# Linear attention: context times output weights first, then queries times the folded weights

## The chip, the cores and the metric

One core of a Trainium2 chip runs the whole program. Its engines work side by side, each through its own queue in order, and meet at semaphores: TensorE (PE; its weight loads are PEld), VectorE (DVE), ScalarE (ACT), GpSimd (POOL) and SyncE (SP). The metric is the device time of one execution in microseconds.

## The reference

A decoder of two layers, on x of shape (2, 1024, 256), that is 2 batches of 1024 tokens and 256 features, all in 32-bit floats. Each layer has a self attention, a cross attention with a small context, and a third part. The change lies in the first part alone, a pre-norm linear attention with 4 heads of 64 and a feed-forward net:

```
h = layer_norm(x, ln1_g, ln1_b)
q, k, v = (h @ wq, h @ wk, h @ wv), each split in 4 heads of 64
q = softmax(q * scale, over the 64 features of the head)
k = softmax(k * scale, over the 1024 tokens)
context = einsum('bhnd,bhne->bhde', k, v)
attn    = einsum('bhnd,bhde->bhne', q, context)
x = x + attn @ wo + bo
h = layer_norm(x, ln2_g, ln2_b)
x = x + gelu(h @ w_ff1 + b_ff1) @ w_ff2 + b_ff2
x = x @ w_d + b_d
```

## The kernel before

The program is written engine by engine: four layer functions, each one block with a list of instructions per engine, in an order set by hand. `linear_attention_layer` is the first of them. It treats the two batches b = 0 and 1 in an interleaved order. Activations lie feature by token: FT = 2 tiles of 128 features, with 1024 tokens in NCH = 2 chunks of 512. Queries and values are made token by feature (4 units u of two 128-token tiles, 256 features each). Each batch has four PSUM banks of 128x512 floats, `bank(b, 0)` to `bank(b, 3)`.

For each batch, the steps between the two norms are:

- `keys` (TensorE), `max_keys` (VectorE, L650), `exp_keys` (ScalarE, L518): the keys, feature by token, and exp of them shifted by their maximum. The exp leaves the sum over tokens in k_s. The division by that sum comes later.
- `values` and `queries` (TensorE, both through `by_token`, L343), copied by `copy_values` (VectorE, L659), or shifted by the maximum of each head (`shift_queries`, VectorE: L665 reduces, L667 subtracts), then `exp_queries` (ScalarE, L524) and `normalise_queries` (VectorE: L673 sum, L675 reciprocal, L677 multiply).
- `turn_keys` (TensorE, L358) transposes exp(keys), and `copy_keys` (ScalarE, L530) moves them to SBUF. `turn_queries` (L376) and `copy_queries` (L537) do the same for the queries, the other way round.
- `contexts` (TensorE, L366): for each of 2 head pairs a 128x128 product over the 1024 tokens. `copy_context` (VectorE, L690) takes the two 64x64 blocks on its diagonal and multiplies them by 1/k_s; the rest of the tile `context` stays zero.
- `attend` (TensorE, L385): context times queries, 4 products of 128x512. `copy_attended` (ScalarE, L544) copies them to SBUF.
- `project` (TensorE, L393): the output weights a_wo times the attended values, 8 products. `add_attended` (VectorE: L698 adds bias and residual, L701 the two halves for the mean).
- The second norm: `mean` (L314), `centre` (L619), `square` (ScalarE, L495), `variance` (L325), `roots` (ScalarE, L509 and L512), `normalise` (VectorE, L626 and L629). For batch 1 the squares are made on VectorE (`fold_squares`, L728 and L730), and `folded_variance` (L319) takes them.
- The feed-forward part runs in units: `widen(u)` (L407), `gelu(u)` (L559, L561), `narrow(u)` (L418), with weights and activations split in a rounded part and a rest, by three products each. ScalarE makes the rounded parts (`split_w` L547, `split_h2` L552), GpSimd the rests (`leave_w` L290, `leave_h2` L295, L307 for the activations). TensorE runs `mean` of batch 1 after widen(2) and `folded_variance` after widen(5).

Every product of plain 32-bit floats appears as two MATMUL instructions in the trace, so 16 products are x32; a transpose of 128x128 and a product of rounded operands (fp32r) appear as one.

The orders that matter here:

- TensorE: ... queries(1), attend(0), turn_keys(1), project(0), turn_queries(1), mean(0), contexts(1), variance(0), attend(1), project(1), widen(0) ...
- VectorE: ... normalise_once(1), copy_context(0), shift_queries(1), normalise_queries(1), add_attended(0), centre(0), copy_context(1), normalise(0), add_attended(1), centre(1) ...
- ScalarE: ... copy_queries(0), exp_queries(1), copy_attended(0), copy_keys(1), split_w(0, 2, 3), copy_queries(1), split_w(1), square(0), roots(0), copy_attended(1), split_h2(0), gelu(0) ...
- GpSimd: leave_w(0, 2, 3, 1), leave_h2(0) for both chunks, then the rests of the activations.

SyncE issues only two loads of later weights in this layer (L282), and they are done well before the stretch of the change.

Of the kernel before, what the change touches and what calls it, by code (L numbers as in the profile page):

```python
# [24 lines left out]
ALU = mybir.AluOpType  # L25
ACT = mybir.ActivationFunctionType
AX = mybir.AxisListType.X

P = 128
B, S, D = 2, 1024, 256  # L30
T = B * S
FT = D // P
CH = 512
NCH = S // CH
TT = S // P
# [64 lines left out]
class Chip:  # L100
# [52 lines left out]
    def bank(self, i):  # L153
        return self.psum[i // 2][:, (i % 2) * CH:(i % 2 + 1) * CH]
# [29 lines left out]
def linear_attention_layer(nc, c):  # L184

    DH = 64
# [10 lines left out]
    with ExitStack() as ctx:  # L197
# [3 lines left out]
        sg = [c.signals(nc, f"a{b}", dict(  # L201
            k_proj=4, k_step=7, k_shift=1, k_exp=4, k_turned=4, k_copied=4, v_proj=4, v_copied=4,
            q_proj=4, q_step=12, q_shift=4, q_exp=4, q_norm=4, q_turned=4, q_copied=4,
            ctx_done=1, ctx_copied=1, at_done=4, at_copied=4, o_done=4, y_done=4,
            y2_done=4, d_done=4)) for b in range(B)]
        ff = c.signals(nc, "ff", dict(done=UNITS, act=2 * UNITS, rest=UNITS, narrowed=FT * UNITS, split=1, left=1, squared=1))
        parts = [("w", i) for i in (0, 2, 3, 1)] + [("h", b, j) for b in range(B) for j in range(NCH)]
# [2 lines left out]
        zeroed = sems.enter_context(nc.semaphore("a_zeroed"))  # L210
# [7 lines left out]
        k_r = sb("a_k_r", [P, B, FT])  # L218
        q_m = sb("a_q_m", [P, B, 4, 8])
        q_s = sb("a_q_s", [P, B, 4, 8])  # L220
        context = sb("a_context", [P, B, FT, P])
# [3 lines left out]
        room = lambda b, i: arenas[b][:, i * FT * S:(i + 1) * FT * S]  # L225
        tiles = lambda b, i: room(b, i).rearrange("p (m t) -> p m t", m=FT)
        h1, h2, centred, squares = ([tiles(b, i) for b in range(B)] for i in range(4))
        ek = qt = [tiles(b, 4) for b in range(B)]
        v_t = [room(b, 3).rearrange("p (t n) -> p t n", t=TT) for b in range(B)]
        ekt_t = [room(b, 2).rearrange("p (t n) -> p t n", t=TT) for b in range(B)]  # L230
        q_t = [room(b, 5).rearrange("p (u n) -> p u n", u=4) for b in range(B)]
        at = [tiles(b, 5) for b in range(B)]
        y = h1
        round_tiles = lambda b, i: arenas_round[b][:, i * FT * S:(i + 1) * FT * S].rearrange("p (m t) -> p m t", m=FT)
        h2_high, h2_rest = ([round_tiles(b, i) for b in range(B)] for i in (3, 1))
# [25 lines left out]
        bank = lambda b, i: c.bank(4 * b + i)  # L261
        col = lambda j: slice(j * CH, (j + 1) * CH)
# [12 lines left out]
        with nc.Block() as block:  # L275
# [34 lines left out]
            def _(pe):  # L310
# [10 lines left out]
                def variance(b, s):  # L321
                    for j in range(NCH):
                        pe.wait_ge(*s["sq"](j + 1))
                        for k in range(FT):
                            mm = pe.matmul(bank(b, 2 * j + 1), c.mean_w[:], squares[b][:, k, col(j)], start=(k == 0), stop=(k == 1))  # L325
                        mm.then_inc(s["var"].sem)
# [23 lines left out]
                def queries(b):  # L350
                    by_token(b, "a_wq", sg[b]["v_copied"], sg[b]["q_proj"])

                def turn_keys(b):
                    for u in range(4):
                        pe.wait_ge(*sg[b]["q_shift"](u + 1))
                        for t in (0, 1):
                            for m in range(FT):
                                mm = pe.transpose(bank(b, u)[:, t * D + m * P:t * D + (m + 1) * P],  # L358
                                                  ek[b][:, m, (2 * u + t) * P:(2 * u + t + 1) * P], c.ident[:])
                        mm.then_inc(sg[b]["k_turned"].sem)  # L360

                def contexts(b):
                    pe.wait_ge(*sg[b]["q_copied"](1))
                    for m in range(FT):
                        for t in range(TT):
                            mm = pe.matmul(bank(b, 0)[:, m * P:(m + 1) * P], ekt_t[b][:, t, m * P:(m + 1) * P],  # L366
                                           v_t[b][:, t, m * P:(m + 1) * P], start=(t == 0), stop=(t == TT - 1))
                    mm.then_inc(sg[b]["ctx_done"].sem)

                def turn_queries(b):  # L370
# [6 lines left out]
                                                  q_t[b][:, u, t * D + m * P:t * D + (m + 1) * P], c.ident[:])  # L377
                        mm.then_inc(sg[b]["q_turned"].sem)

                def attend(b):  # L380
                    pe.wait_ge(*sg[b]["ctx_copied"](1))
                    pe.wait_ge(*sg[b]["q_copied"](4))
                    for j in range(NCH):
                        for m in range(FT):
                            pe.matmul(bank(b, 2 * j + m), context[:, b, m, :], qt[b][:, m, col(j)],  # L385
                                      start=True, stop=True).then_inc(sg[b]["at_done"].sem)

                def project(b):
                    for j in range(NCH):
                        pe.wait_ge(*sg[b]["at_copied"](2 * (j + 1)))  # L390
                        for m in range(FT):
                            for k in range(FT):
                                mm = pe.matmul(bank(b, 2 * j + m), c.w("a_wo", k, m * P, P), at[b][:, k, col(j)],  # L393
                                               start=(k == 0), stop=(k == 1))
                            mm.then_inc(sg[b]["o_done"].sem)

# [53 lines left out]
                values(1)  # L450
                turn_queries(0)
                contexts(0)
                queries(1)
                attend(0)
                turn_keys(1)
                project(0)
                turn_queries(1)
                mean(0, ln2[0])
                contexts(1)
                variance(0, ln2[0])  # L460
                attend(1)
                project(1)
                for n in range(UNITS + LAG):
                    if n < UNITS:
# [26 lines left out]
            def _(act):  # L491
# [14 lines left out]
                def roots(b, s, eps, scale=1.0):  # L506
                    for j in range(NCH):
                        act.wait_ge(*s["var"](j + 1))
                        act.activation(factor(b, j), bank(b, 2 * j + 1), ACT.Ln, bias=eps[:, 0:1], scale=scale).then_inc(s["log"].sem)  # L509
                    for j in range(NCH):  # L510
                        act.wait_ge(*s["log"](j + 1))
                        act.activation(factor(b, j), factor(b, j), ACT.Exp, scale=-0.5).then_inc(s["rstd"].sem)  # L512
# [8 lines left out]
                def exp_queries(b):  # L521
                    for u in range(4):
                        act.wait_ge(*sg[b]["q_shift"](u + 1))
                        act.activation(q_t[b][:, u, :], q_t[b][:, u, :], ACT.Exp, scale=SCALE).then_inc(sg[b]["q_exp"].sem)  # L524

                def copy_keys(b):
                    act.wait_ge(*ln1[b]["once"](NCH))
                    for u in range(4):
                        act.wait_ge(*sg[b]["k_turned"](u + 1))
                        act.activation(ekt_t[b][:, 2 * u:2 * u + 2, :].rearrange("p t n -> p (t n)"), bank(b, u), ACT.Copy)\  # L530
                           .then_inc(sg[b]["k_copied"].sem)
# [5 lines left out]
                        act.activation(qt[b][:, :, u * D:(u + 1) * D], bank(b, u).rearrange("p (m n) -> p m n", m=FT),  # L537
                                       ACT.Copy).then_inc(sg[b]["q_copied"].sem)

                def copy_attended(b):  # L540
                    for j in range(NCH):
                        for m in range(FT):
                            act.wait_ge(*sg[b]["at_done"](2 * j + m + 1))
                            act.activation(at[b][:, m, col(j)], bank(b, 2 * j + m), ACT.Copy).then_inc(sg[b]["at_copied"].sem)  # L544

                def split_w(i):
                    act.activation(w_high[i], w_raw[i], ACT.Copy).then_inc(split["w", i].sem)  # L547

                def split_h2(b):
                    for j in range(NCH):  # L550
                        act.wait_ge(*ln2[b]["out"](FT * (j + 1)))
                        act.activation(h2_high[b][:, :, col(j)], h2[b][:, :, col(j)], ACT.Copy).then_inc(split["h", b, j].sem)  # L552
# [32 lines left out]
                copy_keys(0)  # L585
                copy_queries(0)
                exp_queries(1)
                copy_attended(0)
                copy_keys(1)
                act.wait_ge(c.first_loaded, 48)  # L590
                for i in (0, 2, 3):
# [3 lines left out]
                split_w(1)  # L595
                square(0, ln2[0])
                roots(0, ln2[0], c.eps)
                copy_attended(1)
                split_h2(0)
                for u in range(UNITS):  # L600
                    gelu(u)
# [9 lines left out]
            def _(dve):  # L611
# [66 lines left out]
                           .then_inc(sg[b]["q_norm"].sem)  # L678

                def copy_context(b):  # L680
                    dve.wait_ge(*sg[b]["k_exp"](4))
                    dve.tensor_tensor(k_r[:, b, :], k_s[:, b, :, 0], k_s[:, b, :, 1], ALU.add).then_inc(sg[b]["k_step"].sem)
                    dve.wait_ge(*sg[b]["k_step"](6))
                    dve.reciprocal(k_r[:, b, :], k_r[:, b, :]).then_inc(sg[b]["k_step"].sem)
                    dve.wait_ge(*sg[b]["k_step"](7))
                    dve.wait_ge(zeroed, 1)
                    dve.wait_ge(*sg[b]["ctx_done"](1))
                    for m in range(FT):
                        for h in (0, DH):
                            ins = dve.tensor_scalar(context[h:h + DH, b, m, h:h + DH], bank(b, 0)[h:h + DH, m * P + h:m * P + h + DH],  # L690
                                                    k_r[h:h + DH, b, m:m + 1], None, ALU.mult)
                    ins.then_inc(sg[b]["ctx_copied"].sem)

                def add_attended(b):
                    for j in range(NCH):
# [2972 lines left out]
def wait_for_weights(nc, c):  # L3668

    with nc.Block() as block:  # L3670

        @block.sync
        def _(sync):
            sync.wait_ge(c.first_loaded, 48)
            sync.wait_ge(c.others_loaded, B * 16)


LAYERS = [linear_attention_layer, cross_attention_and_recurrence, causal_attention_layer,
          context_attention_layer]

# [60 lines left out]
```

## Time and profile before

| | |
|---|---|
| time before, median of 3 runs | 1552.42 us (1550.23 to 1552.64) |
| the profiled execution, its own time | 1552.19 us |
| its span (first to last instruction) | 1550.4 us |
| PE busy | 1458.8 us, 94% |
| DVE busy | 988.1 us, 64% |
| ACT busy | 762.3 us, 49% |
| POOL busy | 454.1 us, 29% |
| mean granted TensorE clock | 0.983 of full |
| first layer's attention up to the first widen | 0 to 113.3 us of the span |

Times are counted from the start of the span. Busy shares are averages over all four layer functions. A row of the timeline gives the start, the time until the end of the last of the merged instructions, the engine, the line, what is written and read, the count, and in brackets the idle time of that engine just before it, with what ended it.

### The profile page before, as it was taken

How to read it: one execution, taken by the hardware profiler on the slowest of the kernel's cores; microseconds unless marked ns; L12 is line 12 of the kernel's file. 1: busy time of each engine (PE TensorE's matmuls, PEld its weight loads, DVE VectorE, ACT ScalarE, POOL GpSimd, SP SyncE). 2: the span in 40 equal slices, each digit the busy share in tenths (PEclk: the TensorE clock that was granted, in tenths of full speed). 3: DMA queues.
4: the chain of work that ended last, by engine and by line, in shares of the span. 5: the costliest groups of instructions: out<-in, count | busy, mean ns of one | idle time of the engine just before them, and what ended most of it. 6: DMA issues, size and time to landing. Idle time of an engine off the chain costs nothing. (4 is left out here: it accounts for less than half of the span.)

```text
span 1550.4 us, 19613 instructions
## 1 busy us (share of the span) xinstructions
PE 1458.8 (94%) x7170; PEld 859.1 (55%) x7170; DVE 988.1 (64%) x1506; ACT 762.3 (49%) x1317; POOL 454.1 (29%) x348
## 2 busy tenths in 40 slices
PE   6999999989999899879999999899889999999998
PEld 3757765423232365444545443323568888888886
DVE  5774244778877634448887773677577574664753
ACT  5566345533434642725666665434655544445442
POOL 0046430142221410370000000201236656655562
PEclk9999999999999999989999999999999999999999
DMA  7000000000000000191553300000413222223201
GB/s 292 1 0 0 1 4 1 0 1 1 1 1 0 1 0 1 48 142 16 132 68 50 43 2 1 4 1 0 137 41 106 72 82 100 78 70 107 73 10 55
DMA packets 39047, 67.59 MB, mean 44 GB/s; under 512 B 3944, under 2 KB 19368, under 8 KB 38568
## 3 DMA queue, kind: packets, MB, share of 16 engines
q1 hardware_dynamic: 38952, 66.33, 16.1%
q8 instruction: 58, 0.95, 0.3%
q14 instruction: 37, 0.30, 0.1%
HBM read 57.80 MB, written 8.39 MB: 43 GB/s over the span
## 5 line engine op out<-in xcount | busy, mean ns | idle before, releaser
L2232 ACT ACTIVATE arena<-psum 128x512 f32<-128x512 f32 (+3 forms) x384 | 164.7, 498 | 118.8 <-PE psum L2082 85.1
L2277 DVE TENSOR_REDUCE b_mx<-psum 128x1 f32<-128x512 f32 (+3 forms) x304 | 181.4, 653 | 57.0 <-PE psum L2058 47.4
L3021 POOL TENSOR_TENSOR m_w_rest<-m_w,m_w_high 128x512 fp32r<-128x512 f32 (+1 forms) x88 | 111.6, 1270 | 154.7 <-ACT m_w_high L3220 154.7
L3471 DVE TENSOR_TENSOR m_hidden<-m_gelu,psum 128x512 f32<-128x512 f32 (+1 forms) x88 | 60.4, 686 | 147.7 <-ACT m_gelu L3312 124.5
L3114 PE MATMUL psum<-m_x_high,m_w_high 128*128 128x512 f32 (+1 forms) x352 | 137.9, 392 | 3.2 <-issue 3.2
L3027 POOL TENSOR_TENSOR m_h_rest<-m_hidden,m_h_high 128x512 fp32r<-128x512 f32 (+1 forms) x88 | 122.1, 1388 | 59.0 <-ACT m_h_high L3234 59.0
L3114 PE MATMUL psum<-m_x_rest,m_w_high 128*128 128x512 f32 (+1 forms) x352 | 137.7, 391 | 0.0
L3114 PE MATMUL psum<-m_x_high,m_w_rest 128*128 128x512 f32 (+1 forms) x352 | 137.6, 391 | 0.0
L3312 ACT ACTIVATE m_gelu<-psum 128x512 f32<-128x512 f32 (+1 forms) x88 | 52.4, 596 | 119.7 <-PE psum L3114 119.7
L1359 ACT ACTIVATE x_probs<-psum 128x1024 f32<-128x1024 f32 x56 | 57.3, 1023 | 90.4 <-PE psum L1097 90.4
L1517 DVE TENSOR_REDUCE x_mx<-psum 128x2 f32<-128x1024 f32 x64 | 76.6, 1218 | 35.0 <-PE psum L1071 34.8
L3234 ACT ACTIVATE m_h_high<-m_hidden 128x512 fp32r<-128x512 f32 (+1 forms) x88 | 55.7, 633 | 82.7 <-DVE m_hidden L3471 82.7
L2079 PE MATMUL psum<-b_q_stack,b_k_stack 98*128 98x512 bf16 (+3 forms) x288 | 89.9, 331 | 5.5 <-DMA b_q_stack<-b_stage 3.1
L2055 PE MATMUL psum<-b_k_stack,b_q_stack 96*128 96x512 bf16 (+3 forms) x288 | 87.1, 332 | 4.8 <-DVE b_mx L2277 2.1
L1994 POOL TENSOR_TENSOR weights_sb<-weights_sb 128x1024 f32<-128x1024 f32 x3 | 5.7, 1892 | 271.0 <-DVE weights_sb L2332 271.0
L3114 PEld LDWEIGHTS psum<-m_x_high,m_w_high 128*128 128x128 f32 (+1 forms) x352 | 65.3, 185 | 18.4 <-issue 3.6
L3114 PEld LDWEIGHTS psum<-m_x_high,m_w_rest 128*128 128x128 f32 (+1 forms) x352 | 65.4, 186 | 15.2
L3114 PEld LDWEIGHTS psum<-m_x_rest,m_w_high 128*128 128x128 f32 (+1 forms) x352 | 65.4, 186 | 15.1
L2094 PE MATMUL psum<-arena,weights_sb 128*32 128x512 f32 (+3 forms) x768 | 73.3, 500 | 0.0
L3127 PE MATMUL psum<-m_h_high,m_o_high 128*128 128x512 f32 (+1 forms) x176 | 72.3, 411 | 0.2 <-POOL m_h_rest L3027 0.2
L3127 PE MATMUL psum<-m_h_high,m_o_rest 128*128 128x512 f32 (+1 forms) x176 | 68.8, 391 | 0.0
L3127 PE MATMUL psum<-m_h_rest,m_o_high 128*128 128x512 f32 (+1 forms) x176 | 68.7, 390 | 0.0
(594 smaller groups left out, 3252.7 us busy)
## 6 DMA issues: line engine op xcount, KB each, us to landing
m_w<-w SPq DMA_DIRECT2D x32, 512.0 KB, 4.5
m_wo<-wo SPq DMA_DIRECT2D x16, 512.0 KB, 4.0
weights_sb<-weights SPq DMA_DIRECT2D x2, 2820.0 KB, 12.3
m_w<-w SPq DMA_DIRECT2D x16, 344.0 KB, 4.6
b_q_stack<-b_q_dram SPq DMA_DIRECT2D x36, 128.0 KB, 6.0
b_k_stack<-b_k_dram SPq DMA_DIRECT2D x36, 128.0 KB, 5.9
weights_sb<-weights SPq DMA_DIRECT2D x1, 3328.0 KB, 14.3
b_q_dram<-b_q_parts SPq DMA_DIRECT2D x6, 512.0 KB, 3.4
```

The costliest lines, as they stand in the source:

```text
L1359: ins = act.activation(probs[slot % RING][:], two_heads(units), ACT.Exp, scale=SCALE)
L1517: dve.tensor_reduce(mx[:, n % 2, i // 2, i % 2, :], two_heads(tile(("piece", n, i))), AX, ALU.max).then_inc(s["read"].sem)
L2055: mm = pe.matmul(bank[:, x * keys:(x + 1) * keys], qs[n % 3][0:ROWS, h, qi * P:(qi + 1) * P], ks[n % 3][0:ROWS, h, first:first + keys], st ...
L2079: mm = pe.matmul(score(slot)[:, 0:n], ks[a][0:ROWS + SHIFT, h, ki * P:(ki + 1) * P], qs[a][0:ROWS + SHIFT, h, q0:q0 + n], start=True, stop ...
L2094: mm = pe.matmul(out_tile[h * PAD:(h + 1) * PAD, CH - n:CH], v_aug[:, b * TT + ki, quad * QUAD + h, :], probs[(QUAD * (2 * pair + i) + h) ...
L2232: act.activation(probs[slot % RING][:, 0:n], score(slot)[:, 0:n], ACT.Exp, scale=SCALE).then_inc(s["expd"].sem)
L2277: dve.tensor_reduce(mx[:, part, qi, heads[0]:heads[0] + nh], tile(("piece", p))[:, 0:nh * keys].rearrange("p (h n) -> p h n", n=keys), AX, ...
L3021: pool.tensor_tensor(w_rest[:, n % W_RING, :, :, 0:H_N(n % HT)], raw_of(n), w_high[:, n % W_RING, :, :, 0:H_N(n % HT)].bitcast(F32), ALU.s ...
L3027: pool.tensor_tensor(h_rest[rows, n % H_RING, :], hidden[rows, n % 2, :], h_high[rows, n % H_RING, :].bitcast(F32), ALU.subtract).then_inc ...
L3114: mm = pe.matmul(c.bank(base + n % 2)[0:H_N(h), :], of[:, k, :], x_of[ex % 2][:, k, :], start=(k == 0 and i == 0), stop=(k == FT - 1 and i ...
L3127: mm = pe.matmul(total(m), of[rows, n % O_RING, m * P:(m + 1) * P], h_of[rows, n % H_RING, :], start=(h == 0 and i == 0), stop=(h == HT - ...
L3471: dve.tensor_tensor(hidden[rows, n % 2, :], gelu[rows, n % 2, :], c.bank(2 + n % 2)[rows, :], ALU.mult)\
```

## The change

Before, the queries q are multiplied by the context C and the result by the output weights: (q C) Wo. After, the context is multiplied by the output weights first, and the queries by that product: q (C Wo).

- `contexts` swaps its two operands, so that the context comes out transposed, values by keys.
- `copy_context` copies the four diagonal blocks as they are. Then it forms 1/k_s, waits for `folded`, and writes `fold`, 128x256 for each head pair, from bank(b, 1), multiplied by 1/k_s.
- `attend` and `copy_attended` are gone. `fold_context` takes attend's place on TensorE: two products of 128x256. `project` waits for `fold_copied` and for all of `q_copied`, and takes `fold` as stationary and the queries as moving operand.
- `fold` lies in the first 512 columns of the room that held the attended values.

```diff
@@ contexts
-                            mm = pe.matmul(bank(b, 0)[:, m * P:(m + 1) * P], ekt_t[b][:, t, m * P:(m + 1) * P],
-                                           v_t[b][:, t, m * P:(m + 1) * P], start=(t == 0), stop=(t == TT - 1))
+                            mm = pe.matmul(bank(b, 0)[:, m * P:(m + 1) * P], v_t[b][:, t, m * P:(m + 1) * P],
+                                           ekt_t[b][:, t, m * P:(m + 1) * P], start=(t == 0), stop=(t == TT - 1))
@@ TensorE
-                def attend(b):
+                def fold_context(b):
+
                     pe.wait_ge(*sg[b]["ctx_copied"](1))
+                    pe.wait_ge(*sg[b]["q_copied"](2))
+                    for m in range(FT):
+                        mm = pe.matmul(bank(b, 1)[:, m * D:(m + 1) * D], context[:, b, m, :], c.w("a_wo", m, 0, D),
+                                       start=True, stop=True)
+                    mm.then_inc(sg[b]["folded"].sem)
+
+                def project(b):
+                    pe.wait_ge(*sg[b]["fold_copied"](1))
                     pe.wait_ge(*sg[b]["q_copied"](4))
                     for j in range(NCH):
                         for m in range(FT):
-                            pe.matmul(bank(b, 2 * j + m), context[:, b, m, :], qt[b][:, m, col(j)],
-                                      start=True, stop=True).then_inc(sg[b]["at_done"].sem)
-
-                def project(b):
-                    for j in range(NCH):
-                        pe.wait_ge(*sg[b]["at_copied"](2 * (j + 1)))
-                        for m in range(FT):
                             for k in range(FT):
-                                mm = pe.matmul(bank(b, 2 * j + m), c.w("a_wo", k, m * P, P), at[b][:, k, col(j)],
+                                mm = pe.matmul(bank(b, 2 * j + m), fold[b][:, k, m * P:(m + 1) * P], qt[b][:, k, col(j)],
                                                start=(k == 0), stop=(k == 1))
                             mm.then_inc(sg[b]["o_done"].sem)
@@ order on TensorE
-                attend(0)
+                fold_context(0)
                 turn_keys(1)
                 project(0)
...
-                attend(1)
+                fold_context(1)
                 project(1)
@@ ScalarE
-                def copy_attended(b):
-                    for j in range(NCH):
-                        for m in range(FT):
-                            act.wait_ge(*sg[b]["at_done"](2 * j + m + 1))
-                            act.activation(at[b][:, m, col(j)], bank(b, 2 * j + m), ACT.Copy).then_inc(sg[b]["at_copied"].sem)
...
-                copy_attended(0)
...
-                copy_attended(1)
@@ VectorE
                 def copy_context(b):
+                    dve.wait_ge(zeroed, 1)
+                    dve.wait_ge(*sg[b]["ctx_done"](1))
+                    for m in range(FT):
+                        for h in (0, DH):
+                            ins = dve.tensor_copy(context[h:h + DH, b, m, h:h + DH], bank(b, 0)[h:h + DH, m * P + h:m * P + h + DH])
+                    ins.then_inc(sg[b]["ctx_copied"].sem)
                     dve.wait_ge(*sg[b]["k_exp"](4))
...
                     dve.wait_ge(*sg[b]["k_step"](7))
-                    dve.wait_ge(zeroed, 1)
-                    dve.wait_ge(*sg[b]["ctx_done"](1))
+                    dve.wait_ge(*sg[b]["folded"](1))
                     for m in range(FT):
-                        for h in (0, DH):
-                            ins = dve.tensor_scalar(context[h:h + DH, b, m, h:h + DH], bank(b, 0)[h:h + DH, m * P + h:m * P + h + DH],
-                                                    k_r[h:h + DH, b, m:m + 1], None, ALU.mult)
-                    ins.then_inc(sg[b]["ctx_copied"].sem)
+                        ins = dve.tensor_scalar(fold[b][:, m, :], bank(b, 1)[:, m * D:(m + 1) * D], k_r[:, b, m:m + 1], None, ALU.mult)
+                    ins.then_inc(sg[b]["fold_copied"].sem)
```

## Rows read from the trace of the kernel before

**Rows 1.** The page: busy time, share of span and count per engine.
```profile
PE 1458.8 (94%) x7170; PEld 859.1 (55%) x7170; DVE 988.1 (64%) x1506; ACT 762.3 (49%) x1317; POOL 454.1 (29%) x348
```

**Rows 2.** Timeline of TensorE, 71 to 114 us: start, length, operation, count, idle before.
```profile
71.73 7.07 PE L343 MATMUL psum<-weights_sb,a_arena 128*128 128x256 f32 x32
78.64 3.60 PE L385 MATMUL psum<-arena,a_context 128*128 128x512 f32 x8
82.07 1.91 PE L358 MATMUL psum<-ident,a_arena 128*128 128x128 f32 x16
83.82 7.03 PE L393 MATMUL psum<-arena,weights_sb 128*128 128x512 f32 x16
...
94.42 1.12 PE L314 MATMUL psum<-ln,mean_w 128*128 128x512 f32 x2 [0.96 <-DVE ln L701]
...
102.39 3.60 PE L385 MATMUL psum<-a_arena,a_context 128*128 128x512 f32 x8
106.76 7.13 PE L393 MATMUL psum<-a_arena,weights_sb 128*128 128x512 f32 x16 [0.78 <-ACT a_arena L544]
113.33 1.03 PE L407 MATMUL psum<-arena_round,ln_round 128*128 128x512 f32 x2
```

**Rows 3.** Timeline of VectorE, 51 to 106 us.
```profile
51.09 0.69 DVE L667 TENSOR_TENSOR arena<-psum,a_q_m 128x512 f32<-128x512 f32 x1
51.70 0.68 DVE L665 TENSOR_REDUCE a_q_m<-psum 128x8 f32<-128x512 f32 x1
52.41 0.69 DVE L667 TENSOR_TENSOR arena<-psum,a_q_m 128x512 f32<-128x512 f32 x1
...
64.68 2.63 DVE L659 COPY a_arena<-psum 128x512 f32<-128x512 f32 x4
...
72.03 1.18 DVE L690 TENSOR_SCALAR a_context<-psum,a_k_r 64x64 f32<-64x64 f32 x4 [2.05 <-PE psum L366]
...
79.57 0.69 DVE L667 TENSOR_TENSOR a_arena<-psum,a_q_m 128x512 f32<-128x512 f32 x1
...
85.80 0.69 DVE L677 TENSOR_TENSOR a_arena<-a_arena,a_q_s 128x512 f32<-128x512 f32 x1
...
90.89 0.75 DVE L698 SCALAR_TENSOR_TENSOR arena<-psum,vectors_sb,arena 128x512 f32<-128x512 f32 x1 [0.96 <-PE psum L393]
91.67 2.69 DVE L701 TENSOR_TENSOR ln<-arena 128x512 f32<-128x512 f32 x1
...
105.25 0.75 DVE L626 SCALAR_TENSOR_TENSOR arena<-arena,vectors_sb,ln 128x512 f32<-128x512 f32 x1 [4.82 <-ACT ln L512]
```

**Rows 4.** Timeline of TensorE at folded_variance of batch 1.
```profile
127.28 1.13 PE L319 MATMUL psum<-a_arena,mean_w 128*128 128x512 f32 x2 [1.05 <-DVE a_arena L730]
```

**Rows 5.** Timeline of ScalarE, 80 to 86 us.
```profile
80.29 0.63 ACT L524 ACTIVATE a_arena<-a_arena 128x512 f32<-128x512 f32 x1 [1.10 <-DVE a_arena L667]
80.83 2.04 ACT L544 ACTIVATE arena<-psum 128x512 f32<-128x512 f32 x4
82.77 2.06 ACT L530 ACTIVATE a_arena<-psum 128x512 f32<-128x512 f32 x4
84.69 1.08 ACT L547 ACTIVATE ln_round<-weights_sb 128x1024 fp32r<-128x1024 f32 x1
```

**Rows 6.** GpSimd's timeline and line L290 (shortest, median, longest ns), VectorE's L701.
```profile
85.86 2.87 POOL L290 TENSOR_TENSOR weights_sb_round<-weights_sb,ln_round 128x1024 fp32r<-128x1024 f32 x1 [80.86 <-ACT ln_round L547]
L290 POOL TENSOR_TENSOR weights_sb_round<-weights_sb,a_w_high x2: 2352/2580/2808, 88.7 to 91.5; 128x1024 fp32r<-128x1024 f32 x2
88.24 1.03 DVE L701 TENSOR_TENSOR ln<-arena 128x512 f32<-128x512 f32 x1
```

**Rows 7.** Timeline of GpSimd at the rest of h2, batch 0.
```profile
108.87 2.88 POOL L295 TENSOR_TENSOR arena_round<-arena,arena_round 128x1024 fp32r<-128x1024 f32 x1 [12.03 <-ACT arena_round L552]
```

**Rows 8.** Busy time by stretch: PE, PEld, DVE, ACT, POOL, then granted clock.
```profile
20.00:22.00 2.00, 0.47 (x1) 0.30 (x2) 1.85 (x3) 1.97 (x4) 0.00 (x0) 1.00 0.75 180
22.00:26.00 4.00, 4.00 (x7) 1.66 (x6) 3.89 (x8) 3.60 (x5) 0.00 (x0) 0.57 1.05 451
```

More of the change, by code:

```diff
@@ L203, in linear_attention_layer @@
             q_proj=4, q_step=12, q_shift=4, q_exp=4, q_norm=4, q_turned=4, q_copied=4,
-            ctx_done=1, ctx_copied=1, at_done=4, at_copied=4, o_done=4, y_done=4,
+            ctx_done=1, ctx_copied=1, folded=1, fold_copied=1, o_done=4, y_done=4,
             y2_done=4, d_done=4)) for b in range(B)]
@@ L231, in linear_attention_layer @@
         q_t = [room(b, 5).rearrange("p (u n) -> p u n", u=4) for b in range(B)]
-        at = [tiles(b, 5) for b in range(B)]
+        fold = [room(b, 5)[:, 0:FT * D].rearrange("p (m n) -> p m n", m=FT) for b in range(B)]
         y = h1
```

## The prediction

> **What bounds the kernel now.** Start with the page [rows 1]. TensorE is busy 94% of the span, which suggests that any work taken off it shortens the run. That is an average over four layers; the change touches only the first, so I read that layer's stretch, 64 to 130 us, engine by engine in order of time.
>
> TensorE's own timeline comes first [rows 2]. From 71.73 us its pieces follow each other without idle time through queries(1), attend(0), turn_keys(1) and project(0). Then come two short waits: 0.96 us for DVE's second sum ahead of the ln2 mean, and 0.78 us for ACT's copy of the attended values ahead of project(1). widen(0) follows project(1) at 113.33. So TensorE is the bound here, but others are close behind. VectorE's timeline [rows 3] shows how close: in add_attended(0) DVE waits for TensorE by only 0.96 us, and its second sum L701 ends at 91.67 + 2.69 = 94.36, which releases the mean at 94.42. A chain hangs on that sum: mean, centring, square, variance, roots, normalise(0), the split of h2, widen(0); and on DVE itself add_attended(1) and the squares for folded_variance(1), for which TensorE again waits 1.05 us at 127.28 [rows 4]. From the second sum on, DVE's chain and TensorE's stream are within about 1 us of each other.
>
> **Part by part.** *Removed from TensorE:* attend, 8 instructions of 512 columns per batch. The row of attend(0) runs from 78.64 to the start of turn_keys(1) at 82.07: 3.43 us, twice [rows 2]. *Added:* fold_context, two matmuls of 256 columns, 4 instructions. queries(1) has 32 of that form in 78.64 - 71.73 = 6.91 us [rows 2], 0.216 each, so 0.86 us. Net -2.57 us a batch, -5.1 us in all, if nothing else moved. contexts only swaps its operands, 128 columns either way, and project has the same 16 instructions with another stationary matrix: both cost what they did.
>
> *Removed from ScalarE:* the eight copies of copy_attended, 82.77 - 80.83 = 1.94 us a batch [rows 5]. ACT is not the bound at batch 0; at batch 1 the copies are what project(1) waits for (the 0.78 us).
>
> *VectorE:* four context copies of 64x64 stay (1.18 us for four [rows 3]); copy instead of multiply I cost at nothing, since both read 64 columns of PSUM. They no longer wait for the reciprocal, which is done in time anyway. New are two multiplications 128x256 out of PSUM, a form that the trace does not have. Bounds: 0.30 us apart for 64 columns (1.18 over four) and 0.65 apart for the 512 columns of copy_values (2.63 over four) [rows 3]. The slope between them gives 0.45 each, the value that I take: 0.90 us for the pair, bounds 0.6 to 1.3. The Trainium skill ("VectorE: DVE Perf Modes", the section on the TRN2 errata) gives 120 + 256 cycles at 0.96 GHz, an estimate of 0.39 us each; by that page the sum would be 0.1 us lower.
>
> *The wait.* This is what counts. copy_context(0) now ends with a wait for folded, and fold_context(0) stands on TensorE behind all of queries(1). On DVE shift_queries(1) is queued behind that wait, then normalise_queries(1) and add_attended(0). Before, DVE shifted each quarter of the queries as TensorE delivered it, the last at 79.57 [rows 3]. Now:
> - the fold starts at 78.64, ends at 78.64 + 3 x 0.216 + 0.37 (what the last of queries(1) takes, 7.07 - 31 x 0.216) = 79.67; the pair of multiplications runs 79.70 to 80.60;
> - four quarters of shift_queries(1) at 52.41 - 51.09 = 1.32 us, 0.71 of it the maximum L665 [rows 3]: the last L667 begins at 80.60 + 3 x 1.32 + 0.71 = 85.28, where it began at 79.57: 5.7 us later;
> - turn_keys(1), which needs each quarter, no longer starts at once: it is paced by DVE, its last quarter goes at 86.0, and project(0) starts at about 86.45 instead of 83.82, in spite of the 2.57 us saved. It ends at about 93.4, its second product at 90;
> - normalise_queries(1): its last L677 began 85.80 - 79.57 = 6.23 us after the last L667 [rows 3], four quarters of 1.56. Undisturbed, DVE is through with it at 92.1 (it was at 86.4). add_attended(0) then no longer waits for project(0), and its four products (some 0.77 each) and two sums (some 0.65 each) end at 96.5, 2.1 us later than now;
>
> *The move against GpSimd.* ACT's copy_keys(1) stands behind exp_queries(1), so the splits of the weights move too: before, exp of the last quarter at 80.29, eight copies, split at 84.69, L290 at 85.86 [rows 5, 6]; now exp at 86.0, four copies, first split at 86.0 + 0.54 + 1.92 = 88.5, and GpSimd's first L290 1.17 later, at 89.64. The rows show what happens when a DVE operation with two SBUF inputs meets a GpSimd one [rows 3, 6]: L701 at 91.67 takes 2.69 instead of 0.69 and ends 0.55 us after GpSimd's third L290 (91.5 + 2.35), while GpSimd's second, at 88.68, takes 2.81 because L701 of 88.24 is running. One waits for the other to finish. The skill has the same rule ("SBUF — State Buffer", "Who interferes with whom"): such a DVE instruction and a GpSimd instruction that reads SBUF hold the same port in turn. Before, the queries were normalised before GpSimd began at 85.86 (one L677 at its edge). Now they are not. I alternate the two queues, each L290 2.35 us alone and 2.22 after a DVE operation, each DVE operation 0.55 after a release:
> - L290 first 89.64 to 92.0; the third L677, due at 89.96, ends at 92.55 (L290 comes first by 0.3 us);
> - L290 second to 94.77; the fourth L677, due 93.41, ends at 95.32;
> - L290 third to 97.54; first L701, due 96.78, ends at 98.09;
> - L290 fourth, ready at 97.7, to 100.31; second L701, due 99.56, ends at 100.86.
> The second sum is thus 100.86 - 94.36 = 6.5 us later.
>
> *After the sum.* The chain through mean, contexts(1), variance, roots and normalise(0) is unchanged and moves by 6.5. For batch 1 the wait for folded(1) is covered: the fold follows variance(0) (102.39 before), DVE has its product 2.0 us later, at 104.4 in old time, and it would idle until 105.25 anyway [rows 3]; if that cover failed, normalise(0) would pay the difference. project(1) starts at 104.4 in old time instead of 106.76, 2.3 us sooner; but widen(0) needs GpSimd's rest of h2, ready at 108.87 + 2.88 = 111.75 [rows 7], so only 113.33 - 111.75 = 1.6 us are gained at widen(0), and TensorE gives them back at the mean and folded variance of batch 1, which hang on DVE's chain. I put 0 of them in the sum, bound -1.6. Nothing later in the kernel waits for a clock of its own, so the shift stays to the end.
>
> Sum, against the profiled execution's 1552.19 us (span 1550.4 and 1.8 around it; the median is 0.2 above): 1552.19 + 6.5 = 1558.7 us.
>
> **Rivals.**
> - *B, the port costs less.* If the third L677 wins against the first L290 (0.3 us decide), the second sum comes 4.8 us late: 1557.0. With no collisions at all it is 2.1: 1554.3, no change that can be told. For it: the margin is small. Against it: both starts hang on the same L667, so it does not scatter much. Less the up to 1.6 of widen(0), this case spans 1553 to 1557.
> - *C, the clock falls as well.* In 20 to 22 us TensorE was busy for 0.47 us of 2, at 2.4 GHz; in the 4 us that follow, full of work, the granted clock is 0.57 on average, that is mostly at 1.2 GHz [rows 8]. In the new order TensorE has little to do from 79.7 to 86.4 and again from 94.8 to 100.9. A fall in the first stretch slows project(0), which has some 3 us of cover (its second product is needed at 96). A fall in the second slows contexts(1), which the variance waits for. In the 4 us of the row 0.43 x 4 = 1.7 us of clock were lost: 1560.4. Against it: both stretches hold short pieces of work.
> - *D, faster.* TensorE's stream sets the end and the wait is absorbed: 1552.19 - 5.1 = 1547.1. It takes a DVE that is ahead of TensorE by more than the stall. DVE waited for project(0) by 0.96 us [rows 3]; the stall of 5.7 us would have to be under about 1.3. It would need the fold to be released before the end of queries(1), against TensorE's order. The change not doing what it says gives a time within this case and the old one.
>
> **How the numbers follow.** Forecast 0.57, B 0.22, C 0.16, D 0.05. The forecast's own range is 1557 to 1560 (0.3 on either side for the new DVE operation, -1.6 for widen(0), and for GpSimd's queue falling otherwise in the feed-forward part). For 8 in 10 I reach down to most of B, 1555.0, and up over C, 1561.5. A measurement of this kernel can tell about 0.2%, 3.1 us, from no change. Faster by more: D without the failed-to-apply part, 0.04. Within: B's end without collisions and the rest of D, 0.11. Slower: 0.85.
>
> **What would show it.** In the profile of the changed kernel: DVE idle about 6 us before its first 128x256 multiplication, released by the fold; turn_keys(1) in four pieces 1.32 us apart; the third and fourth L677 near 2.6 and 1.9 us instead of 0.69, and GpSimd's L290 beginning near 89.6; the second L701 ending near 100.9; project(1) following the fold by about 1 us without ACT between. The prediction is wrong if shift_queries(1) starts before 79 us, if L677 and L290 overlap without growing, or if TensorE does not wait for DVE's two sums between 94.8 and 101.

## The result and the profile after

The changed kernel takes 1561.47 us (median of 6 runs, 1558.44 to 1565.27) against 1552.26 us for the kernel before in the same comparison. The ratio is 1.0064, with a 95% interval of 1.0051 to 1.0077: 0.64% slower, or 1.0064 x 1552.2 = 1562.1 us. The forecast was 1558.7 us. Its direction, the wait and the collisions hold; the loss is 9.9 us where 6.5 were forecast, because TensorE's clock fell twice and the sum had no term for it.

The profiled execution took 1564.93 us with a span of 1562.0 us, 11.6 more than before. TensorE's timeline at the change, the rows that answer to [rows 2]:

```profile
71.82 7.07 PE L343 MATMUL psum<-weights_sb,a_arena 128*128 128x256 f32 x32
78.73 1.03 PE L385 MATMUL psum<-weights_sb,a_context 128*128 128x256 f32 x4
82.11 0.66 PE L358 MATMUL psum<-ident,a_arena 128*128 128x128 f32 x4 [2.36 <-DVE a_arena L661]
83.44 1.11 PE L358 MATMUL psum<-ident,a_arena 128*128 128x128 f32 x4 [0.67 <-DVE a_arena L661]
...
87.00 8.67 PE L395 MATMUL psum<-arena 128*128 128x512 f32 x16
95.50 1.91 PE L376 MATMUL psum<-ident,a_arena 128*128 128x128 f32 x16
98.17 1.12 PE L314 MATMUL psum<-ln,mean_w 128*128 128x512 f32 x2 [0.76 <-DVE ln L698]
102.22 2.07 PE L314 MATMUL psum<-ln,mean_w 128*128 128x512 f32 x2 [2.92 <-DVE ln L698]
104.08 5.30 PE L366 MATMUL psum<-a_arena 128*128 128x128 f32 x32
109.22 3.60 PE L325 MATMUL psum<-arena,mean_w 128*128 128x512 f32 x8
112.65 1.03 PE L385 MATMUL psum<-weights_sb,a_context 128*128 128x256 f32 x4
114.72 7.13 PE L395 MATMUL psum<-a_arena 128*128 128x512 f32 x16 [1.04 <-DVE a_arena L688]
```

Up to 78.73 nothing has changed. The fold takes four instructions where attend took eight. Then turn_keys(1), which had run through in one piece, comes in pieces, each behind an L661 of DVE (the old L667); the first piece takes 0.66 us, the second, with the same work, 1.11. project(0) takes 8.67 us where it took 7.03, and contexts(1) 5.30 where it took 3.73. Both wear the mark of a slower TensorE. Before, contexts(1) and the variance behind it were:

```profile
95.38 3.73 PE L366 MATMUL psum<-a_arena 128*128 128x128 f32 x32
98.95 3.60 PE L325 MATMUL psum<-arena,mean_w 128*128 128x512 f32 x8
```

VectorE's timeline, which answers to [rows 3]; L661 is the old L667, L667 the old L673, L671 the old L677, L698 the old L701:

```profile
79.86 0.87 DVE L688 TENSOR_SCALAR arena<-psum,a_k_r 128x256 f32<-128x256 f32 x2 [6.46 <-PE psum L385]
80.66 0.68 DVE L659 TENSOR_REDUCE a_q_m<-psum 128x8 f32<-128x512 f32 x1
...
85.34 0.69 DVE L661 TENSOR_TENSOR a_arena<-psum,a_q_m 128x512 f32<-128x512 f32 x1
...
90.01 2.58 DVE L671 TENSOR_TENSOR a_arena<-a_arena,a_q_s 128x512 f32<-128x512 f32 x1
92.51 0.67 DVE L667 TENSOR_REDUCE a_q_s<-a_arena 128x8 f32<-128x512 f32 x1
...
93.45 1.89 DVE L671 TENSOR_TENSOR a_arena<-a_arena,a_q_s 128x512 f32<-128x512 f32 x1
...
96.70 1.42 DVE L698 TENSOR_TENSOR ln<-arena 128x512 f32<-128x512 f32 x1
98.04 1.40 DVE L695 SCALAR_TENSOR_TENSOR arena<-psum,vectors_sb,arena 128x512 f32<-128x512 f32 x2
99.47 2.69 DVE L698 TENSOR_TENSOR ln<-arena 128x512 f32<-128x512 f32 x1
```

DVE idles 6.46 us for the fold. The third and fourth L671 take 2.58 and 1.89 us, and both sums are drawn out too, the second to 99.47 + 2.69 = 102.16. GpSimd's timeline, which answers to [rows 6], shows what they meet:

```profile
89.67 2.36 POOL L290 TENSOR_TENSOR weights_sb_round<-weights_sb,ln_round 128x1024 fp32r<-128x1024 f32 x1 [84.67 <-ACT ln_round L543]
92.00 5.57 POOL L290 TENSOR_TENSOR weights_sb_round<-weights_sb,a_w_high 128x1024 fp32r<-128x1024 f32 x2
99.28 2.34 POOL L290 TENSOR_TENSOR weights_sb_round<-weights_sb,arena_round 128x1024 fp32r<-128x1024 f32 x1 [1.71 <-ACT arena_round L543]
```

And the busy time by stretch (columns as in [rows 8]) has the clock: 0.50 of full, the lower level of 1.2 GHz, in two stretches just behind or among TensorE's waits for DVE.

```profile
80.00:84.00 4.00, 1.22 (x7) 0.98 (x8) 3.91 (x7) 1.22 (x2) 0.00 (x0) 0.93 0.00 0
84.00:88.00 4.00, 3.58 (x13) 2.26 (x12) 3.88 (x7) 2.62 (x6) 0.00 (x0) 0.50 0.00 0
102.00:106.00 4.00, 3.78 (x11) 2.75 (x12) 2.64 (x5) 1.41 (x2) 0.00 (x0) 0.50 0.00 0
```

To tell parts of a few us from each other, I read each profile between two marks: the first instruction behind queries(1) on TensorE (attend(0) or the fold, "the mark"), and the first DVE product that takes the feed-forward total of batch 0 (L705 before, L702 after). What lies ahead of the mark varies by 2.3 us from profile to profile (the mark lies between 76.44 and 78.73); the mean clock of whole runs varies too (0.975 to 0.985 of full). Two profiles of the changed kernel ("after" and "after_again") differ by 0.2 us in these readings. Before and after, the second mark is:

```profile
147.60 1.44 DVE L705 SCALAR_TENSOR_TENSOR arena<-psum,vectors_sb,arena 128x512 f32<-128x512 f32 x2 [0.92 <-PE psum L418]
```
```profile
157.98 1.46 DVE L702 SCALAR_TENSOR_TENSOR arena<-psum,vectors_sb,arena 128x512 f32<-128x512 f32 x2 [0.89 <-PE psum L420]
```

That is 147.60 - 78.64 = 68.96 us before and 157.98 - 78.73 = 79.25 after: 10.3 us of the loss lie here, against 9.9 for whole runs. All runs, with those two readings (each from one profile, less the kernel before) beside the ratio of whole runs:

| run | second sum ends, from the mark | between the marks | ratio [95%] |
|---|---|---|---|
| before | 15.72 | 68.96 | 1 |
| after | +7.7 | +10.3 | 1.0064 [1.0051, 1.0077] |
| after_again | +7.6 | +10.1 | 1.0063 [1.0048, 1.0078] |
| hold | +2.7 | +3.5 | 1.0029 [1.0017, 1.0041] |
| move | +0.9 | +3.7 | 1.0021 [1.0011, 1.0030] |
| both | -3.0 | -2.9 | 0.9987 [0.9975, 0.9998] |
| fill | +6.4 | +6.5 | 1.0041 [1.0028, 1.0054] |
| fold0_only | +7.5 | +9.9 | 1.0056 [1.0038, 1.0074] |
| fold1_only | 0.0 | +0.1 | 0.9992 [0.9976, 1.0009] |
| before_hold | -2.0 | -1.3 | 0.9994 [0.9984, 1.0005] |
| both_later | -3.0 | -5.3 | 0.9973 [0.9959, 0.9988] |
| before_hold_later | -2.0 | -2.6 | 0.9975 [0.9960, 0.9990] |

### The profile page after: what moved, and what is told of

It is laid out like the page before. It is cut to its first block and busy times, and to the rows that moved or that the text cites. A ratio compares the mean times of both kernels' runs of the same rounds, so it can differ in the third digit from the quotient of the medians.

```text
span 1562.0 us, 19593 instructions
## 1 busy us (share of the span) xinstructions
PE 1462.1 (94%) x7158; PEld 861.6 (55%) x7162; DVE 992.9 (64%) x1510; ACT 758.0 (49%) x1309; POOL 453.5 (29%) x348
```

## The experiments

Theory: the changed kernel loses by DVE's wait for the fold, by the collisions between DVE and GpSimd into which this wait pushes them, and by TensorE's clock. Rivals: one of the three does it alone, or the loss lies elsewhere.

**The changed kernel again**, as the mark for its neighbours.

> The changed kernel once more, as the mark beside which the next three are read. Its trace so far has the second sum of the second norm ending at 102.2 us (94.4 before) and the clock at 1.2 GHz in two stretches, 83 to 90 and 101 to 107 us. Theory (the DVE wait, the port shared with GpSimd, and the clock together): 1558 to 1565 us in single runs, middle near 1561. Rival (what was first seen was a chance state of the clock in that one profile): middle at 1557 or below.

Measured: 1562.97 us, ratio 1.0063. Its profile has both collisions and both stretches at 1.2 GHz again, so they were not a chance of the first profile.

**hold**: GpSimd starts on the weights only after both sums.

```diff
+                pool.wait_ge(*ln2[0]["sum"](NCH))
                 for i in (0, 2, 3, 1):
                     leave_w(i)
```

> The changed kernel, with GpSimd's four subtractions for the weights held back until DVE has made both sums ahead of the second norm (one wait more on GpSimd, nothing left out). DVE still waits for the fold. Theory: no L677 or L701 takes over 0.8 us; the last quarter of the queries is normalised at 92.1 instead of 95.3, the second sum ends near 97 instead of 102.2; TensorE is not idle for long before the mean, so the second fall of the clock goes too: 1555 us, 6 less than the changed kernel. Rival (the port costs nothing on the path, the wait alone does it): 1561, as the changed kernel. Second rival (the subtractions are now late for widen(0)): over 1561.

Measured: 1556.48 us, 6.5 less than the changed kernel beside it (6 expected). VectorE's timeline, then TensorE's:

```profile
90.54 0.69 DVE L672 TENSOR_TENSOR a_arena<-a_arena,a_q_s 128x512 f32<-128x512 f32 x1
...
94.58 0.75 DVE L696 SCALAR_TENSOR_TENSOR arena<-psum,vectors_sb,arena 128x512 f32<-128x512 f32 x1 [0.65 <-PE psum L396]
95.37 0.69 DVE L699 TENSOR_TENSOR ln<-arena 128x512 f32<-128x512 f32 x1
```
```profile
85.96 8.59 PE L396 MATMUL psum<-arena 128*128 128x512 f32 x16
94.38 1.91 PE L377 MATMUL psum<-ident,a_arena 128*128 128x128 f32 x16
96.13 1.88 PE L315 MATMUL psum<-ln,mean_w 128*128 128x512 f32 x4
97.85 3.73 PE L367 MATMUL psum<-a_arena 128*128 128x128 f32 x32
```

DVE's products and both sums are back at 0.69. The first fall of the clock is still there (project(0) 8.59 us), and DVE now waits 0.65 us for it; that is why the second sum is 2.7 us late and not the 2.1 worked out. The second fall is gone, and with it TensorE's waits at the means. Holding GpSimd back thus takes off 6.8 of the 10.3 us. Not all of that is the change's own: the kernel before has collisions too [rows 6], and the run "before_hold" below shows that the same edit takes 1.3 us off it between the marks.

**move**: DVE scales the fold of batch 0 after it has shifted the queries of batch 1.

```diff
                 copy_context(0)
                 shift_queries(1)
+                scale_fold(0)
                 normalise_queries(1)
...
                 copy_context(1)
+                scale_fold(1)
```

(scale_fold is the end of copy_context, from the wait for folded on.)

> The changed kernel, with the two multiplications of the fold of batch 0 moved behind shift_queries(1) on DVE (batch 1 as it was; nothing left out). Theory: DVE shifts each quarter as TensorE delivers it, the last at 79.6; the fold is scaled at 80.3 to 81.1; turn_keys(1) has no gaps and the first stretch at 1.2 GHz is gone. GpSimd's subtractions now begin 2 us sooner than in the kernel before, near 83.9, and meet the third and fourth L677 and both sums: second sum near 95.4, 1.1 later than before: 1553. Rival (with the wait gone, the 5 us that TensorE saves show in full): 1547.

Measured: 1554.94 us, expected 1553. VectorE, GpSimd and TensorE:

```profile
83.96 1.91 DVE L671 TENSOR_TENSOR a_arena<-a_arena,a_q_s 128x512 f32<-128x512 f32 x1
...
86.74 1.90 DVE L671 TENSOR_TENSOR a_arena<-a_arena,a_q_s 128x512 f32<-128x512 f32 x1
```
```profile
82.83 2.49 POOL L290 TENSOR_TENSOR weights_sb_round<-weights_sb,ln_round 128x1024 fp32r<-128x1024 f32 x1 [77.84 <-ACT ln_round L543]
```
```profile
80.18 7.03 PE L395 MATMUL psum<-arena 128*128 128x512 f32 x16
...
91.45 1.12 PE L314 MATMUL psum<-ln,mean_w 128*128 128x512 f32 x2 [2.11 <-DVE ln L699]
94.21 2.08 PE L314 MATMUL psum<-ln,mean_w 128*128 128x512 f32 x2 [1.63 <-DVE ln L699]
96.08 5.51 PE L366 MATMUL psum<-a_arena 128*128 128x128 f32 x32
```

Without the wait the first fall is gone (project(0) 7.03), and the second sum is only 0.9 late, as forecast (1.1). The collisions remain: taking ACT's eight copies away lets GpSimd begin sooner (82.83 - 77.57 = 5.26 us from the mark, where it was 85.86 - 78.64 = 7.22), and it meets L671 twice. What the expectation missed is again the clock: TensorE, 2.11 and 1.63 us idle at the means, takes 2.08 us for the second of them and 5.51 for contexts(1). So the 5 us that TensorE saves come to nothing even with the wait gone; the rival of 1547 falls.

**both** edits together.

> The changed kernel with both edits of the two before it: the fold scaled behind shift_queries(1), and GpSimd held back until both sums are made. Theory: the second sum ends near 91.7, 2.7 us before that of the kernel before, and widen(0) starts about 109; the chain on DVE sets the end: 1549. Rival (the TensorE stream sets the end): 1547. Rival (what the changed kernel loses lies elsewhere, in the clock of the later layers for instance): 1555 or above.

Measured: 1549.21 us, ratio 0.9987. VectorE's second sum and TensorE:

```profile
88.48 0.69 DVE L700 TENSOR_TENSOR ln<-arena 128x512 f32<-128x512 f32 x1
```
```profile
89.22 1.12 PE L315 MATMUL psum<-ln,mean_w 128*128 128x512 f32 x2 [0.54 <-DVE ln L700]
90.19 3.73 PE L367 MATMUL psum<-a_arena 128*128 128x128 f32 x32
93.76 3.60 PE L326 MATMUL psum<-arena,mean_w 128*128 128x512 f32 x8
```

Neither fall of the clock (1.00 in every stretch of 2 us from 70 to 114), no drawn-out operation up to the second sum, and that sum 3.0 us sooner than before (2.7 expected). The wait and the collisions, with the clock that falls behind them, explain the loss in full: without them the same fold takes 2.0 us less than the kernel before in whole runs, 2.9 between the marks. TensorE's project(0) and contexts(1) take 7.03 and 3.73 us here as they did before, so the swapped operands cost nothing.

**fill**: products on TensorE that nobody reads, in the idle stretches of the changed kernel.

```diff
+                    if b:
+                        pe.wait_ge(*sg[0]["q_copied"](4))
+                        fill(bank(0, 2), 2, CH)
                     for u in range(4):
+                        if b and u:
+                            fill(bank(0, 2), 1, CH // 2)
                         pe.wait_ge(*sg[b]["q_shift"](u + 1))
...
                 turn_queries(1)
+                pe.wait_ge(*sg[1]["q_copied"](2))
+                fill(bank(1, 1), 2, CH)
...
+                    if j == 0:
+                        fill(bank(0, 1), 2, CH)
```

> The changed kernel, with idle-time products on TensorE whose results nobody reads: two of 128x512 and three of 128x256 in the gaps of turn_keys(1), two of 128x512 behind turn_queries(1), two between the two means of the second norm. Nothing is left out. They end before the operand that TensorE waits for is ready, or at most some 0.5 us after. Theory: the granted clock stays at 2.4 GHz from 80 to 108 us; project(0) takes 7.0 us instead of 8.7, so GpSimd's fourth subtraction and the second sum end 1.3 us sooner, near 100.9; the second mean and contexts(1) are 2.6 us shorter. In all 3.9 us less than the changed kernel in the same stretch: 1558.5. Rival (the clock is not on the path): 1562.5. Rival (the clock falls anyway, since such products do not count): over 1562.5.

Measured: 1559.0 us, ratio 1.0041, 3.4 us less than the changed kernel (3.9 expected); +6.5 between the marks. TensorE, then the stretches:

```profile
84.95 7.03 PE L404 MATMUL psum<-arena 128*128 128x512 f32 x16
...
97.51 1.88 PE L355 MATMUL psum<-xT,mean_w 128*128 128x512 f32 x4
99.31 1.13 PE L473 MATMUL psum<-ln,mean_w 128*128 128x512 f32 x2
100.28 3.73 PE L375 MATMUL psum<-a_arena 128*128 128x128 f32 x32
```
```profile
84.00:88.00 4.00, 3.77 (x14) 1.87 (x13) 3.86 (x8) 3.57 (x7) 0.00 (x0) 1.00 0.00 0
100.00:104.00 4.00, 4.00 (x35) 3.76 (x34) 1.74 (x3) 3.25 (x3) 0.00 (x0) 1.00 0.01 4
```

The clock stays at 2.4 GHz (1.00 in every stretch of 2 us from 70 to 114). DVE's wait of 6.46 us and its products of 2.57 and 1.90 us are those of the changed kernel. Here the forecast's sum can be read without the clock: the second sum is 6.4 us late (6.5 worked out), and the second mark 6.5. The clock is the rest, 10.3 - 6.5 = 3.8 us. In whole runs the intervals of the two ratios overlap a little (1.0028 to 1.0054 and 1.0048 to 1.0078), so the size rests on the profiles: 6.5 against 10.3 and 10.1.

**The change for one batch alone.** For the other batch attend, copy_attended and the old project and copy_context stand.

> The change for batch 0 alone; batch 1 attends and projects as in the kernel before. Theory: the whole loss is here, DVE's wait for the fold, the collisions with GpSimd and both falls of the clock: 1561.5 to 1562.5, as the changed kernel. Rival (each batch costs its share): about 1557.

> The change for batch 1 alone; batch 0 attends and projects as in the kernel before. Theory: DVE's wait for the fold lies in time in which it was idle; project(1) starts 1 us after the fold and widen(0) 1.6 us sooner, but the sums of batch 1 on DVE start no sooner, so that TensorE waits longer at the mean and at the folded variance of batch 1: 0 to -0.8 us in all, 1551.8. Rival (what TensorE saves shows): 1549.8. Rival (the wait costs at batch 1 as well): over 1554.

Measured: batch 0 alone 1.0056, batch 1 alone 0.9992 (1550.47 us, not to be told from the kernel before). The whole loss comes from batch 0. TensorE with the change at batch 1 alone:

```profile
102.99 7.13 PE L420 MATMUL psum<-a_arena 128*128 128x512 f32 x16 [1.04 <-DVE a_arena L740]
110.34 0.73 PE L434 MATMUL psum<-arena_round,ln_round 128*128 128x512 f32 x2 [0.22 <-POOL arena_round L297]
```
```profile
117.66 1.12 PE L316 MATMUL psum<-ln,mean_w 128*128 128x512 f32 x2 [1.45 <-DVE ln L750]
```

widen(0) starts 110.34 - 77.19 = 33.15 us from the mark; in the kernel before it is 113.33 - 78.64 = 34.69 [rows 2]. That is 1.5 us sooner where 1.6 were forecast, with GpSimd's rest of h2 as what comes last. At the mean of batch 1 TensorE waits 1.45 us for DVE, and between the marks nothing is left (+0.1).

**before_hold**: the kernel before, with GpSimd held back. This asks whether the gain of "both" is the fold's.

> The kernel before, with GpSimd's four subtractions held back until both sums are made, one wait more. Theory: the collisions that the kernel before already has (L701 of 1.03 and 2.69 us) go; the second sum ends near 92.3 instead of 94.4, but turn_queries(1) holds TensorE until 92.4 anyway, so contexts(1) starts only 1.2 us sooner: 1551. Rival (the held subtractions come too late for widen(0)): over 1552.5.

Measured: 1552.18 us, ratio 0.9994, no change that can be told; 1.3 us between the marks, as expected. It saves less than "both" there (1.3 against 2.9), so of the 2.9 us only 1.6 are the fold's. In whole runs the two ratios, 0.9994 and 0.9987, can't be told apart.

**both_later and before_hold_later**: in addition, the mean and the folded variance of batch 1 come one unit later on TensorE.

```diff
-                    if n == 2:
+                    if n == 3:
                         mean(1, ln2[1])
-                    if n == 5:
+                    if n == 6:
                         folded_variance(1, ln2[1])
```

> The changed kernel with the fold of batch 0 scaled behind shift_queries(1) and GpSimd held back, and in addition the mean and the folded variance of batch 1 one unit of the feed-forward part later on TensorE (after widen(3) and widen(6) instead of widen(2) and widen(5)). Theory: what batch 1 gains is lost in TensorE's waits for DVE at these two places (1.43 us at the mean, 1 to 2 at the folded variance); one unit later they are covered, and about 2 us more are gained: 1547. Rival (gelu and its ring of five tiles set the pace there): 1549, as without the edit.

> The kernel before with the same two edits that do not touch the fold: GpSimd held back, and the mean and folded variance of batch 1 one unit later. It tells how much of a gain over the kernel before is the fold's. Theory: 1.2 us from the held subtractions, 1 from the wait at the folded variance: 1550, 3 us above the folded kernel of the same edits. Rival (the fold saves nothing even so): equal to that kernel.

Measured: with the fold 1548.82 us (1547 expected), ratio 0.9973; without it 1549.23 us (1550 expected), ratio 0.9975. TensorE with the fold:

```profile
114.11 2.21 PE L315 MATMUL psum<-ln,mean_w 128*128 128x512 f32 x4
...
123.11 1.88 PE L320 MATMUL psum<-a_arena,mean_w 128*128 128x512 f32 x4
```

No wait of note is left at either place, and both_later beats the kernel before by 0.27% and, by the two ratios, the changed kernel by 0.9%. Between the marks the fold is worth 5.3 - 2.6 = 2.7 us, near the 3 expected, in one profile of each. Whole runs do not show it: 0.9973 and 0.9975 are what the rival, equal times, expected, but with 0.15% (2.3 us) either way on each they don't exclude the 2.7 us either. Whether the later layers lose them or chance hides them stays open.

## Why the prediction came out as it did

**Bound and chain.** Right. TensorE's 94% was no guide; the chain through DVE's second sum sets the start of everything behind it. The variance of the second norm starts 20.31 us from the mark before (98.95) and 30.49 after (109.22), 10.2 us later, and the second mark moves by 10.3.

**Removed and added.** The fold is 4 instructions in 0.86 us, as costed. The two multiplications of DVE are 80.66 - 79.86 = 0.80 us from the first to the next operation, where my slope gave 0.90. The Trainium skill's 120 + 256 cycles ("VectorE: DVE Perf Modes", the TRN2 errata) was nearer, with an estimate of 0.39 us each. Between the two, the forecast differs by 0.1 us. The four copies of the context, put at the same cost as the multiplications, took 0.93 us instead of 1.18.

**The wait.** Right in place and size. DVE waited 6.46 us. The last subtraction of the shift began 85.34 - 78.73 = 6.61 us from the mark, where 85.28 - 78.64 = 6.64 was worked out. The run "move" shows that the order on DVE makes this wait and not the fold.

**The collisions.** Right: 2.58 and 1.89 us for the two products, the first GpSimd subtraction at 89.67 (89.64 worked out), the first sum ended at 98.12 (98.09). "hold" shows that it is no side effect. Rival B, its cheaper form, did not come.

**The step that failed is the clock.** The sum held no term for it, and rival C was given 16%, one fall with 1.7 us at most, and "against it: both stretches hold short pieces of work". In the profile the clock fell in both stretches, and the short pieces did not hold it up. The first fall came behind the first piece of turn_keys(1): 0.66 us, then 1.11 for the second. The trace of the kernel before has a like case just ahead of [rows 8], which the prediction did not use: TensorE was busy 0.00 us from 18 to 20 us, then come the 0.47 us of [rows 8] from 20 to 22, then the clock fell; here it is 0.00 from 80 to 82 and 1.22 from 82 to 84. Each fall also lasted longer than the one in [rows 8]: by stretches of 2 us some 6.8 us at 1.2 GHz, from about 83.4 and again from about 100.5, against 3.4 there (0.43 x 4 / 0.5). In the work on the path that cost project(0) 8.67 - 7.03 = 1.6 us, contexts(1) 5.30 - 3.73 = 1.6, the second mean 0.9 (from its start to contexts(1) 1.86 us, before 0.96). I also called the first fall covered. It was covered for DVE's first products; but turn_queries(1) follows project(0), ACT's fourth split follows that, GpSimd's fourth subtraction came at 99.28 instead of 97.7, and the second sum, which waits for it, ended at 102.16 instead of 100.86. So 6.5 us became 10.3: 1.3 by the second sum, 2.5 by mean and contexts(1). "fill" takes away the falls and gets the 6.5 back, with the second sum 1.3 us sooner than in the changed kernel. C with both falls priced in full would have given 1552.19 + 10.3 = 1562.5, and the range ended at 1561.5, below the 1562.1 that the ratio gives (the plain median, 1561.47, lies at its very end).

**Batch 1.** Right: covered wait, 1.5 us gained at widen(0) and given back at DVE's next sums.

**Rival D**, faster, needed the fold free of the wait. Even then ("move") the gain did not come, since GpSimd's subtractions moved along with the copies that ACT no longer makes, and the clock fell once behind the means. With those gone too ("both") 2.0 us of the 5.1 showed, and part of those belong to the subtractions held back ("before_hold").

## What to carry to other kernels

A step that is cheaper on the busiest engine can cost more by the wait that it puts into another engine's queue: ask what stands behind that wait, and whether it can be moved behind what does not need it. Work that DVE's operations collide with, as GpSimd's here, is a part of the order too: when one queue slides by 6 us, look at what it now runs beside. And where a forecast leaves TensorE idle in pieces, look in the trace of before for a stretch as empty and what the clock did behind it, and price the slower clock for what follows, with its followers, as part of the likeliest case and not as an accident.

## What the runs showed of the hardware

- TensorE's clock fell behind stretches that were not empty. Between 80 and 84 us of the changed kernel it was busy for 1.22 of 4 us, its longest gap 2.36 us, and 84 to 88 ran at 1.2 GHz; in "move" it fell behind gaps of 2.11 and 1.63 us with one mean between them. With products that nobody reads in the gaps it stayed at 2.4 GHz, and the kernel was some 3.4 us faster for doing more.
- DVE's reduction with one SBUF input did not wait for GpSimd: in the changed kernel the L667 at 92.51 us took 0.67 us, with GpSimd's second and third L290 occupying 92.00 to 97.57.
